# A mixture-of-experts way back in bf16 parts, its slot masks fetched by DMA, on one Trainium2 core

## The reference

```
# first FFN: each of 8 experts takes the k = 128 tokens of a batch with the highest probability
g, m = top_k(probs.transpose(0, 2, 1), 128)          # per batch and expert
h = gelu(x[m] @ w1[e]) @ w2[e]                       # 128 -> 512 -> 128
out[m] += g * h                                      # scattered back to the tokens and added
x = x + gb * out
# second layer: layernorm, modulation, query/key/value, rotary tables,
# 16 heads of 8 numbers, relative positions, causal softmax, ...
```

## Time and profile before

| | |
|---|---|
| median of 3 runs | 2181.04 us (2179.69 to 2186.57) |
| profiled execution, own time | 2186.56 us |
| its span, first to last instruction | 2184.8 us |
| mean granted TensorE clock | 0.959 of full speed |
| busy | PE 87%, DVE 60%, POOL 37%, ACT 32% |
| the stretch that the change touches | 988 us (first `up0`) to 1233 us (first scores of the second attention) |

### The profile page before, as it was taken

One profiled execution on the slowest core, in us unless ns is written; L12 is line 12 of the kernel. 1 busy time (PEld: TensorE's weight loads), 2 busy tenths in 40 slices (PEclk: granted clock), 3 DMA queues, 4 the chain that ended last, 5 costly groups with the idle time before them and its releaser, 6 DMA issues.

```text
span 2184.8 us, 74365 instructions
## 1 busy us (share of the span) xinstructions
PE 1889.9 (87%) x33712; PEld 1398.4 (64%) x33712; DVE 1305.5 (60%) x2440; ACT 691.2 (32%) x1041; POOL 818.5 (37%) x747
## 2 busy tenths in 40 slices
PE   5789999999989889879999989798887988888894
PEld 3567777777767666656652467676666666667784
DVE  2667777777777788777425555565645556454224
ACT  1233333333333233234310133242332333234331
POOL 3356555555555555330203033132232313113442
PEclk9999999999999999999999899998998999899997
DMA  9400000000000000030001231321313213114566
GB/s 303 144 2 2 2 2 2 2 2 1 2 1 2 2 2 2 2 98 1 1 3 25 50 77 33 73 68 35 79 35 76 59 44 75 28 50 128 176 200 189
DMA packets 81035, 113.33 MB, mean 52 GB/s; under 512 B 9485, under 2 KB 63505, under 8 KB 80288
## 3 DMA queue, kind: packets, MB, share of 16 engines
q1 hardware_dynamic: 71952, 97.95, 16.7%
q0 software_dynamic: 4544, 8.54, 1.1%
q10 hardware_dynamic: 4224, 2.10, 0.4%
HBM read 83.25 MB, written 45.68 MB: 59 GB/s over the span
## 4 chain that ended last, share of the span: by engine, by line
PE 48%; DVE 13%; issue 6%; ACT 2%; DMA 2%; POOL 1%; another core or an unknown queue 1%; SPq 0%; POOLq 0%; DVEq 0%; ACTq 0%
PE psum L1095 45%; DVE colmax L1969 2%; DVE colmax L1800 1%; DMA arena<-in_pack 1%; DVE rowmax L1977 1%; PE psum L1438 1%; ACT arena L1568 1%; DVE ctx_sum L1828 1%; DVE arena L1773 1%; DVE raw L1788 1%; PE psum L1166 1%; PE psum L1158 0%; DVE stats L1762 0%; ACT prob L1553 0%
## 5 line engine op out<-in xcount | busy, mean ns | idle before, releaser
L1095 PE MATMUL psum<-arena 128*32 128x32 f32 (+8 forms) x10680 | 749.5, 256 | 83.6 <-issue 52.9
L1095 PEld LDWEIGHTS psum<-arena 128*32 128x32 f32 (+3 forms) x10680 | 549.6, 128 | 209.3 <-issue 127.7
L1568 ACT ACTIVATE arena<-psum 128x1024 f32<-128x1024 f32 (+1 forms) x192 | 169.5, 883 | 356.5 <-PE psum L1095 286.6
L1800 DVE TENSOR_REDUCE colmax<-psum 128x512 bf16<-128x2048 f32 (+2 forms) x96 | 168.2, 1752 | 126.0 <-PE psum L1095 126.0
L1969 DVE TENSOR_REDUCE colmax<-psum 128x256 bf16<-128x768 f32 (+2 forms) x160 | 178.3, 1115 | 88.3 <-PE psum L1095 62.1
L1095 PE MATMUL psum<-neg_ident,rowmax 128*32 128x128 bf16 (+2 forms) x4864 | 217.0, 243 | 10.7 <-issue 9.5
L1583 ACT COPY ctx_sum<-psum 128x384 f32<-128x384 f32 x128 | 61.3, 479 | 496.4 <-PE psum L1095 496.4
L1977 DVE TENSOR_REDUCE rowmax<-psum 128x2 bf16<-128x256 f32 (+1 forms) x192 | 98.0, 511 | 183.0 <-PE psum L1095 171.7
L2216 POOL TENSOR_TENSOR arena<-ctx_sum 128x256 f32<-128x256 f32 x128 | 109.0, 852 | 252.8 <-DVE ctx_sum L1828 241.6
L1095 PE MATMUL psum<-prob,ffw 128*32 128x128 f32 x5120 | 169.6, 279 | 24.2 <-DVE rowmax L1806 24.1
L1095 PEld LDWEIGHTS psum<-prob,ffw 128*32 128x32 f32 x5120 | 134.6, 111 | 79.7 <-DVE rowmax L1806 53.8
(11 more groups left out here) (266 smaller groups left out, 2711.1 us busy)
## 6 DMA issues: line engine op xcount, KB each, us to landing
arena<-in_pack SPq DMA_DIRECT2D x39, 578.0 KB
sent<-in_empty SPq DMA_DIRECT2D x9, 2112.0 KB, 35.2
arena<-qk_parts SPq DMA_DIRECT2D x96, 128.0 KB
q_copies<-arena SPq DMA_DIRECT2D x32, 256.0 KB
prob<-q_copies SPq DMA_DIRECT2D x128, 64.0 KB, 3.5
qk_parts<-arena SPq DMA_DIRECT2D x16, 384.0 KB, 3.4
arena<-sent SPq DMA_DIRECT2D x39, 132.0 KB
ffw<-in_L_w SPq DMA_DIRECT2D x1, 2048.0 KB, 10.1
```

The lines of the kernel that those rows point to most:

```text
L1095: return pe.matmul(o, lhsT, rhs, start=start, stop=stop, skip_group_check=True)
L1568: act.activation(probs_of(i)[:, :, h0 * P:(h0 + nh) * P], slot(n)[:, 0:(i + 1) * W].rearrange("p (j c) -> p j c", c=W), ACT.Exp, scale=HD1 ...
L1800: dve.tensor_reduce(colmax[:, n % 2, :], scores_of(u).rearrange("p j c -> p c j"), AX.X, ALU.max).then_inc(colmax_dve, 1)
```

## The change

Four things are changed.

1. **Places by DMA.** `pos_bf` is written to DRAM in the first FFN (`places_out`). Eight transfers `places(b)` of 1 MB each read one batch's eight rows and repeat them on 128 partitions, into three buffers that lie over w1 and w2. The bf16 product that copied a row to 128 partitions is gone. DVE's comparison reads bf16 from SBUF and writes `back` in bf16. `places(b)` for b >= 3 waits until the comparisons of batch b-3 are done.
2. **Outputs in three bf16 parts.** Behind each FFN round stands a new step `y_split`: DVE writes the gated output whole, ACT rounds it to bf16, DVE takes the rest, ACT rounds the rest, DVE takes what is left. `back` multiplies three bf16 products in place of one f32 product.
3. **Closer steps.** `center`, `norm`, key and query all stand behind batch 1. The key's transfers stand behind batch 3 (before: 2), behind `places(6)` and ahead of `places(7)`.
4. **Swapped places.** The query's stack lies where the third parts are, so its six transfers wait until all 64 rounds of `back` are done; the key's stack doesn't.

```diff
@@ the FFN rounds (in both halves)
             add("down0", r=r)
+            add("y_split", r=r)
             for f in choose[0:5]:
                 f()
...
                 slots_transposed()
+                add("places_out")
@@ the way back
-        ahead = [(tokens_a, stat_a), (center_a,), (norm_a, key_a), (query_a,), (), (), (), ()]
+        ahead = [(tokens_a, stat_a), (center_a, norm_a, key_a, query_a), (), (), (), (), (), ()]
+        for b in range(3):
+            add("places", b=b)
         add("late_tables")
...
                 add("back", b=b, x=x)
+            if b + 3 < B:
+                add("places", b=b + 3)
             for f in ahead[b]:
                 f()
                 finish_rotations()
-            if b == 2:
+            if b == 3:
                 keys_out(0)
@@ SP
+                    elif s.kind == "places":
+                        b = s["b"]
+                        w.wait_ge(d_pos, 32)
+                        if b == 0:
+                            w.wait_ge(hid_done, FC * (E + HALF))
+                        elif b == 1:
+                            w.wait_ge(y_done, E + HALF)
+                        elif b == 2:
+                            w.wait_ge(hid_done, FC * 2 * E)
+                        else:
+                            w.wait_ge(back_ready, E * (b - 2))
+                        sp.dma_start(places[b % 3].rearrange("p x s -> p (x s)"),
+                                     pos_dram[b // HALF, b % HALF * E:(b % HALF + 1) * E, :].rearrange(
+                                         "(a x) s -> a (x s)", a=1).partition_broadcast(P)).then_inc(d_places[b % 3], 16)
...
                         if b < 2:
                             w.wait_ge(y_done, 2 * E)
+                            w.wait_ge(backed, B * E if what == "query" else 0)
@@ PE
-                    elif k == "slots":
...
-                        mm(psum[:, r % 4, :], ident_bf[0:rows, r % rows:r % rows + 1].to_broadcast([rows, P]),
-                           pos_bf[:, r // rows, :], start=True).then_inc(slots_full, 1)
...
+                        w.wait_ge(y_ready, hb * E + x + 1)
...
-                        mm(psum[:, ko, :], xin[:, x, b, :], back[:, r % BACKS, :], start=(x == 0),
-                           stop=(x == E - 1)).then_inc(backed, 1)
+                        for c in range(3):
+                            ins = mm(psum[:, ko, :], y_part(hb, x, c)[:, b % HALF, :], back[:, r % BACKS, :],
+                                     start=(x + c == 0), stop=(x == E - 1 and c == 2))
+                        ins.then_inc(backed, 1)
@@ ACT
+                    elif k == "y_split":
+                        r = s["r"]
+                        hb, x = divmod(r, E)
+                        for c in range(2):
+                            if c:
+                                w.wait_ge(y_rest, r + 1)
+                            else:
+                                w.wait_ge(y_done, r + 1)
+                            act.copy(y_part(hb, x, c), y_whole[r % 2].rearrange("p (b d) -> p b d", d=D)).then_inc(
+                                y_cast, 1)
@@ DVE
+                    elif k == "y_split":
...
+                        w.wait_ge(y_cast, 2 * r + 1)
+                        dve.tensor_tensor(whole, whole, y_part(hb, x, 0), ALU.subtract).then_inc(y_rest, 1)
+                        w.wait_ge(y_cast, 2 * r + 2)
+                        dve.tensor_tensor(y_part(hb, x, 2), whole, y_part(hb, x, 1), ALU.subtract).then_inc(y_ready, 1)
...
-                        w.wait_ge(slots_full, r + 1)
-                        dve.tensor_scalar(back[:, r % BACKS, :], psum[:, r % 4, :], iota_col[:, 0:1], None,
+                        w.wait_ge(d_places[b % 3], 16 * (b // 3 + 1))
+                        dve.tensor_scalar(back[:, r % BACKS, :], places[b % 3][:, x, :], iota_col[:, 0:1], None,
                                           ALU.is_equal).then_inc(back_ready, 1)
```

More of the change, by code:

```diff
@@ L295, in build @@
         back_at = attention_at - E
-        back = arena[:, back_at:back_at + BACKS * S].rearrange("p (a s) -> p a s", a=BACKS)
+        back = arena[:, back_at:back_at + BACKS * S // 2].bitcast(BF16).rearrange("p (a s) -> p a s", a=BACKS)
         slot_gate = carve([B, E])
@@ L303, in build @@
                  for a in (rope_b, raw)]
+        y_whole = [ctx_sum[:, z, 0, :] for z in range(2)]
+        y_low = arena[:, 0:E * B * CAP // 2].bitcast(BF16).rearrange("p (h x s) -> p h x s", h=2, x=E)
+        places = [ffw[:, k * 2 * D * E:(k + 1) * 2 * D * E].bitcast(BF16).rearrange("p (x s) -> p x s", x=E)
+                  for k in (0, 2, 1)]
         tables_at = ARENA - TABLES1
@@ L391, in build @@
         both = carve([B, 2, NT, D])
+        pos_dram = nc.dram_tensor("places", (2, HALF * E, S), BF16, kind="Internal").ap()
         parts_dram = nc.dram_tensor("qk_parts", (B, 2, P, 3, S), BF16, kind="Internal").ap()
@@ L399, in build, with y_part @@
         x_tok = t["x"].rearrange("b (n p) d -> p (b n) d", p=P)
+        def y_part(hb, x, c):
+            if c == 2:
+                a = y_low[:, hb, x, :]
+            else:
+                a = xin[:, x, 4 * hb:4 * hb + 4, :].rearrange("p b s -> p (b s)").bitcast(BF16)[:, c * S:(c + 1) * S]
+            return a.rearrange("p (b d) -> p b d", d=D)
         def tokens_of(L, which, b):
@@ L955, in build @@
                                    "gate_done"))
-        up_full, hid_done, down_full, y_done, slots_full, back_ready, backed, x1_ready = (
-            semaphore(n) for n in ("up_full", "hid_done", "down_full", "y_done", "slots_full", "back_ready", "backed",
-                                   "x1_ready"))
+        up_full, hid_done, down_full, y_done, y_cast, y_rest, y_ready, back_ready, backed, x1_ready = (
+            semaphore(n) for n in ("up_full", "hid_done", "down_full", "y_done", "y_cast", "y_rest", "y_ready",
+                                   "back_ready", "backed", "x1_ready"))
+        d_pos = semaphore("d_pos")
+        d_places = [semaphore(f"d_places{k}") for k in range(3)]
         band_ready, band_full, band_done, slots_chosen = (
@@ L1008, in _ @@
                             sp.dma_start(rel0_row, t["rel_emb"][0:1, :].partition_broadcast(P)).then_inc(d_w1, 16)
+                    elif s.kind == "places_out":
+                        w.wait_ge(aux_drained, drained(sel_at[1]))
+                        for half in range(2):
+                            sp.dma_start(pos_dram[half], pos_bf[:, half, :]).then_inc(d_pos, 16)
+                    elif s.kind == "places":
[12 more added lines that the diff above has]
+                                         "(a x) s -> a (x s)", a=1).partition_broadcast(P)).then_inc(d_places[b % 3], 16)
                     elif s.kind == "late_tables":
```

18 lines of the change are left out of this document (9 added, 9 removed).

## The result

The changed kernel takes 2203.12 us (median of 4 runs, 2195.01 to 2205.52), the kernel before 2180.36 beside it (4 runs). The ratio is 1.0101, 95% interval 1.0080 to 1.0122: 22 us slower by the ratio, where 10 were forecast. The measured median lies near the upper end of the stated range (2175 to 2206), and the loss is more than twice the forecast one. On a second chip the same pair gave 1.0106 (1.0071 to 1.0141).

A forecast was written before the change was run, and what follows sets the result against it. It took PE, never resting, to bound the kernel, with DVE already slower in the search's rounds. +19 us in the FFN and -9.1 behind it gave +9.9 us, a forecast median of 2191 us, range 2175 to 2206.

The forecast's parts named there:

- the 1.6 us for clock and late one-hot matrices: FFN's first half: PE's half clock after rests and a late gather of batch 5, on top of DVE's 17.4 us.
- Part 1: FFN: splits add 2.8 us of DVE per first-half round, 19 us in all; the second half hides all but the last.
- Part 2: Way back: a round falls from 1.37 to 0.66 us, less a late start, slow clock and the first batch's steps.
- Rival A: FFN: the splits are hidden behind the search and cost nothing, sum -9.1 us, 2172; chance 0.12.
- The hole: Way back, batch 2: DVE stands in the first batch's steps, no comparison for 17.6 us, PE rests some 10 us.
- with 0.47 a batch costs DVE 4.5 us: Way back: at 0.47 us a comparison DVE needs less per batch than PE's 5.3 us, so PE sets the pace.
- Part 3: Transfers: places(7) late, then the query's stacks uncovered; first scores at 96.6 us after the FFN, 9.1 us gained to the maxima.
- The queue step: SP's queue: places(7) waits behind the key's stacks and lands at 73.3 us after the FFN; PE rests 5 us.
- The 12.5 us row: Profile sign for queueing: a qload behind the query's stacks took up to 12.5 us to land, median 3.5.
- The last term: End of the way back: 0.6 us from first scores at 96.6 to column maxima at 97.2 us after the FFN.
- B: Way back: no clock loss and no queueing behind the stacks, 13.6 us better, 2177, no measurable change; chance 0.26.
- C: Way back: the repeated loads or DVE's comparisons set the pace, +12 us, 2203; chance 0.12.

The follow-up runs named there:

- e6: Changed kernel with the first half's splits made in the second half's rounds, beside those rounds' own: 2103.02 us, 0.9967 of the kernel before.
- e3: Changed kernel with the first batch's steps spread over batches 1, 2 and 3 as before: 2111.23 us, 1.0030 of the kernel before.
- e8: Changed kernel with POOL kept busy in batch 5 of the way back by products that nothing reads: 2119.17 us in a single execution.
- e10: Changed kernel without the loads of places, PE copying rows into PSUM as before, first batch's steps spread: 2136.27 us, 1.0115 of the kernel before.
- e2: Changed kernel with the key's transfers behind places(7) in SP's list: 2121.43 us, 1.0083 of the kernel before.
- e5: Kernel before with only the loads of places and the comparison from SBUF, outputs and products f32, no splits: 2082.88 us, 0.9885.
- e9: Changed kernel, first half's splits moved to the second half, first batch's steps spread, query's stacks not waiting for the last round: 2084.37 us, 0.9884.

## Why the prediction was wrong, step by step

The direction and the two places of loss and gain were right; the size was off by more than a factor of two: +22 for +9.9. Two sums failed. The FFN lost 22.3 us for 19, because the 1.6 us for clock and late one-hot matrices were too little. The way back won 3.6 us for 9.1, and these 5.5 us have three parts. The last `back` came 2.5 us late: the comparison was priced at 0.47 us throughout and takes 1.0 beside POOL, and that delay was passed on to `places(7)`. The query's stacks added 1.0, and the step from the first scores to the maxima 2.0. The last 3.3 us of the miss lie in no stage of the profiles.

**Part 1, the splits: forecast +19, measured +22.3; right in kind.** Spacing 10.7 for 10.8, PE waiting for ACT ahead of `up0` (3.42 and 1.72 us in the profile), second half hidden. e6 shows the whole of it to come from the splits in the search's rounds. The term that was mis-sized is the 1.6 us put on top of 17.4 for clock and late one-hot matrices. DVE's last one-hot matrices end 22.3 us later, counted from the first `up0`. Two of that are the four groups themselves, 26.3 us in place of 24.3 (6.55, 4.62, 6.55 and 6.57 before), which now run beside POOL's work at other moments; 3.2 us are DVE's idle time before 1078.38, where it waits for a `gather` that began after a rest of 5.08 us and took 7.73 us for 5.34. So about 5 us stand where the sum had 1.6. Rival A, that the splits are hidden, is refuted.

**Part 2, the rounds.** First `back` at t = 8.4 (7.8), end of batch 1 at 22.9 (23.5), DVE's return at 41.2 (41.1). That these agree is in part luck: the start was 0.6 us late, the slow clock behind `band` cost some 2.0 us and not 2.9 (24 products in 7.26 us), and from batch 1's end to DVE's return it was 18.3 us and not 17.6. The hole is there all the same, and e3 shows the price of having the steps together, 15.6 us. The forecast had the hole, but it took the closer steps as given and never priced them against the steps apart. What failed is the step behind them: "with 0.47 a batch costs DVE 4.5 us". The mean is right (64 comparisons took 455 ns each), but it is a mean of 0.35 and 1.0, and the 1.0 fall where DVE has the whole delay to make good. `places(6)` was issued after this at 52.4 and not 50.2, the key's stacks at 58.9 and not 56.1, and batch 6 ended at 70.1 (68.7).

The Trainium skill has the rule that I passed over, "SBUF — State Buffer", sections "SBUF: two separate sides" and "Who interferes with whom": DVE and GpSimd share one pair of ports, a DVE instruction in a two-port mode locks it for its whole length, and the later one waits. The traces agree in that the comparison from SBUF and POOL's products go one for one (1.11 us each in e8), and that the one from PSUM is not slowed (e10). Which mode the comparison ran in no trace shows.

**Part 3, the transfers.** The queue step held in size too: `places(7)` took 15.66 us from issue to landing, 15 in the sum. (The 12.5 us row was a weaker sign than I took it for: of the eight `qload` behind the query's stacks the first landed in 3.2 us.) It landed at 76.8 and not 73.3, for the most part because it was issued nearly 3 us later, behind the slow comparisons; PE's rest ahead of batch 7 was 7.27 us for 5, and e2 removes it. Last `back` at 84.3 (81.8): of the load's 3.5 us 2.5 are left, because the clock took only 1.6 us in batch 7 and not 2.9. The query's stacks landed 15.6 us after their first issue (1232.05 to 1247.61), where the sum had 14.8 with the barrier; first scores at 100.1 (96.6). The last term was plainly mis-sized: 0.6 us from first scores to maxima. It was 1.9 before (1231.29 to 1233.19) and 2.6 now, at half clock (0.50 from 1247 to 1251).

**Rivals B and C.** B needs no clock loss and no queueing, and both are there (e2, and PE's 6.95 us for batch 7's 5.3). C, the loads or comparisons as the pace, came out on the measured time (2203) and not in kind, which is luck. In batches 2 and 3 the comparisons did hold the rounds back, and batch 6 ended 1.4 us later than forecast, but e5 has the same loads and slower comparisons (8.64 us for eight beside POOL) and is, with e9, the fastest of all. I argued too little from this side: the sum set a round of 1.37 us against 0.66 and never asked how much of the gain was the row copy's and how much the parts'. Places alone bring a round from 1.37 to 0.86; the parts bring it from there to 0.65, and that last step buys nothing, because the first batch's own chain then ends later than the rounds (e9).

What stays open: the 3 us between the stages' 18.7 and the medians' 22; how DVE's time, ACT's order and PE's slow clock share the FFN's 22.3 us; and whether the stage can end before 78 us, with the query's parts and transfers ahead of the key's, which was not tried.

## What to carry to other kernels

Before a stage's products are made cheaper, find what ends behind them: here a chain of one batch's small steps and two sets of slow transfers ended some 80 us behind the FFN, and faster products didn't end the stage sooner. Work added to an engine should be placed where that engine is idle, not where its operand is born: the same splits cost 22 us in one half and nothing in the other. And when a change has several parts, run each alone: one of this change's four was worth 25 us by itself, and with the other three the kernel was 47 us slower than with it alone (medians on two chips; the ratios say the same).

## What the runs showed of the hardware

- DVE's comparison of 128x512 bf16 from SBUF takes 0.35 us alone (0.49 with an f32 result) and 1.0 to 1.1 us while POOL works on SBUF; from PSUM (f32) it takes 0.75 us either way (e8, e5, e10).
- Four one-hot comparisons of 128x1024 (two inputs in SBUF) take 4.62 us without POOL and 5.5 to 7.5 with POOL's products beside them, and POOL's own product grows from 1.16 to as much as 2.2 us.
- A 1 MB load that repeats 8 KB on 128 partitions landed in a median of 5.0 us, and in 15.66 us when issued behind six transfers of 128 KB to 8 partitions each, half of its packets starting only when theirs were through.
- When PE came back from rests of some 7 us its granted clock was 0.50, the lower level of 1.2 GHz, and later 1.00, the upper level of 2.4 GHz: 0.50 from 1189 to 1193 and 1.00 from 1195 to 1199; 0.50 from 1225 to 1227 and 1.00 from 1229 to 1231. From 1239 to 1249, where PE waited for the stacks most of the time, it was 0.50. Over the way back, rests counted in, the mean was 0.95 before, 0.78 in the changed kernel and 0.98 with places alone.
